# A third segment of layer 0 turned by VectorE, and the long rows put last

## The reference

```python
e = concat(u, i)                      # x through small weights, by rows
h = adj @ (adj.T @ e)                 # layer 0
x = layernorm(x + layernorm(h) * gamma + beta + x)
T1 = adj @ x ; T2 = 2 * (adj @ T1) - x ; T3 = 2 * (adj @ T2) - T1      # layer 1
out = layernorm(x + x @ W0 + T1 @ W1 + T2 @ W2 + T3 @ W3 + bias)
```

## Time and profile before

| | |
|---|---|
| median of three runs | 1171.82 us |
| profiled execution | 1168.52 us, span 1166.7 us |
| TensorE busy | 1082.1 us, 93% |
| VectorE busy | 910.0 us, 78% |
| ScalarE busy | 330.9 us, 28% |
| GpSimd busy | 265.8 us, 23% |
| read from memory | 338.48 MB, 291 GB/s over the span |
| granted TensorE clock | mean 0.992 of full |

### The profile page before, as it was taken

The page is one execution under the profiler, slowest core; times in us unless marked ns, Lnnn a source line. Parts: engine busy times, 40 slices in busy tenths (PEclk is TensorE's granted clock), DMA queues, the critical chain, the costliest instruction groups (busy, mean ns, idle before and its releaser), DMA issues.

```text
span 1166.7 us, 13999 instructions
## 1 busy us (share of the span) xinstructions
PE 1082.1 (93%) x5050; PEld 467.6 (40%) x5050; DVE 910.0 (78%) x942; ACT 330.9 (28%) x592; POOL 265.8 (23%) x428
## 2 busy tenths in 40 slices
PE   6898999999999999868889999999899999988897
PEld 5454444444544544412333333443334444422332
DVE  2797788999989989898777767655577877678885
ACT  1555546645655654501111111000110000001111
POOL 0475735644534533610000000000000000001110
PEclk9999999999999999999999999999999999989999
DMA  9999999999999996999999999999599999999991
GB/s 284 273 292 288 285 278 319 301 297 292 270 287 296 273 284 174 224 298 346 278 347 345 327 322 322 296 288 261 163 319 347 337 335 348 338 282 346 343 333 30
DMA packets 366970, 340.33 MB, mean 292 GB/s; under 512 B 17500, under 2 KB 365700, under 8 KB 366932
## 3 DMA queue, kind: packets, MB, share of 16 engines
q1 hardware_dynamic: 257972, 232.24, 70.7%
q10 hardware_dynamic: 106496, 105.00, 31.0%
q0 software_dynamic: 2464, 2.59, 0.9%
HBM read 338.48 MB, written 1.31 MB: 291 GB/s over the span
## 4 chain that ended last, share of the span: by engine, by line
PE 55%; DVE 13%; SPq 12%; ACT 10%; issue 5%; ACTq 1%; POOL 1%; DMA 1%; DVEq 0%; POOLq 0%
PE bank L1267 26%; ACT terms L842 9%; SPq L378 7%; DVE turned L557 6%; PE bank L1335 5%; SPq L367 5%; PE bank L1280 5%; PE bank L1095 2%; PE bank L1135 2%; PE bank L1123 2%; PE bank L1107 2%; DVE shared L577 2%; PE bank L1147 2%; ACTq L321 1%; PE bank L1313 1%
## 5 line engine op out<-in xcount | busy, mean ns | idle before, releaser
L433 POOL COPY raw<-raw 32x512 f32<-32x512 f32 x320 | 195.3, 610 | 241.5 <-DVE raw L594 201.6
L1267 PE MATMUL bank<-turned,terms 128*128 128x512 f32 x528 | 235.5, 597 | 3.2 <-DVE turned L557 2.7
L577 DVE STREAM_TRANSPOSE shared<-shared 32x512 f32<-32x512 f32 x320 | 224.0, 700 | 4.1
L1095 PE MATMUL bank<-shared 128*64 128x256 f32 x1600 | 207.0, 387 | 10.3 <-DMA shared<-in_adj 10.3
L557 DVE STREAM_TRANSPOSE turned<-shared 128x2048 f32<-128x2048 f32 x70 | 160.2, 2301 | 62.4 <-PE bank L1267 34.2
L557 DVE STREAM_TRANSPOSE turned<-raw 128x2048 f32<-128x2048 f32 x70 | 159.7, 2296 | 52.7 <-PE bank L1267 37.4
L842 ACT COPY terms<-terms 32x512 f32<-32x512 f32 x312 | 192.2, 616 | 5.0 <-DVE terms L587 0.9
L326 POOL DMA_DIRECT2D out<-scratch x32 | 17.4, 551 | 597.2 <-DVE scratch L789 597.0
L1267 PEld LDWEIGHTS bank<-turned,terms 128*128 128x128 f32 x528 | 97.9, 190 | 131.1 <-issue 129.1
L1095 PEld LDWEIGHTS bank<-shared 128*64 128x64 f32 x1600 | 112.8, 137 | 92.0 <-issue 33.7
L1335 PE MATMUL bank<-turned,terms 128*64 128x512 f32 x360 | 97.0, 603 | 21.9 <-DVE turned L557 21.9
(11 more groups left out here) (158 smaller groups left out, 1085.7 us busy)
## 6 DMA issues: line engine op xcount, KB each, us to landing
shared<-in_adj SPq DMA_DIRECT2D x100, 1024.0 KB, 10.6
raw<-in_adj SPq DMA_DIRECT2D x100, 512.0 KB, 10.8
raw<-in_adj ACTq DMA_DIRECT2D x100, 512.0 KB, 12.9
shared<-in_adj SPq DMA_DIRECT2D x100, 512.0 KB, 10.5
shared<-in_adj ACTq DMA_DIRECT2D x100, 512.0 KB, 12.3
raw<-in_adj SPq DMA_DIRECT2D x80, 256.0 KB, 7.6
shared<-in_x SPq DMA_DIRECT2D x5, 256.0 KB, 4.7
xq<-in_x POOLq DMA_DIRECT2D x40, 32.0 KB, 6.0
```

The source lines that it names most:

```text
L433: last = nc.gpsimd.tensor_copy(moved[Q32 * c:Q32 * (c + 1), :, :, Q32 * q:Q32 * (q + 1)], beside[Q32 * q:Q32 * (q + 1), :, c, :, :])
L577: last = nc.vector.transpose(low_turned[Q32 * c:Q32 * (c + 1), :, :, Q32 * q:Q32 * (q + 1)], low[Q32 * q:Q32 * (q + 1), :, :, Q32 * c:Q32 ...
L1095: last = nc.tensor.matmul(t_bank[H * odd:H * (odd + 1), 0:PW], e[:, s * SB + b, :], panels[slot][:, s * SB + b, :], start=(k == 0 and b < ...
L1267: last = nc.tensor.matmul(sum_bank[parity][:, :], terms[:, c * GB + i, columns], turned[place][:, i * BANK:(i + 1) * BANK], start=(first a ...
```

## The change

Segment 1 becomes `THIRD`, and `TILED` becomes 1. The segment is no longer turned by TensorE nor read a second time. VectorE turns it in one instruction per panel (`turn_third`, after `ACROSS`, in place of `turn_last_tile` in every second panel). ScalarE moves blocks 0 to 7 (`move_third`, after the sixteen of `spread_across` and before `keep_t`), GpSimd blocks 8 to 15 (`help_third`, after `move_beside`). TensorE multiplies it in four matmuls at the end of the panel (`add_h_third`), where two `turn_blocks`, two `add_h` and, per two panels, four `add_h_tile` are gone. Its buffers are `raw[1]` and `turned[1]`, so the first load of layer 1 waits for both movers. The segment is loaded again at VectorE's signal. After the last panel ScalarE makes all sixteen spread moves, and GpSimd moves its half of `THIRD` ahead of `BESIDE`. In the second sweep the rows 7 and 8, of eight tiles each, come last instead of early. The second sweep has the same tiles and windows.

```diff
-        TILED = BESIDE
+        TILED = THIRD
-        ROWS3 = [0, 7, 9, 8, 1, 6, 2, 5, 4, 3]
+        ROWS3 = [0, 9, 6, 1, 2, 5, 4, 3, 7, 8]
-        LAST_LOW = [(7, 3), None, (7, 2), (7, 1), (7, 0), (9, 0), (8, 3), (8, 2), (8, 1), (8, 0), (1, 0),
-                    (6, 2), (6, 1), (6, 0), (2, 0), (5, 2), (5, 1), (5, 0), (4, 1), (4, 0), (3, 1), (3, 0)]
+        LAST_LOW = [(6, 2), None, (6, 1), (9, 0), (6, 0), (1, 0), (5, 2), (2, 0), (5, 1), (5, 0), (4, 1), (4, 0),
+                    (3, 1), (3, 0), (7, 3), (7, 2), (7, 1), (7, 0), (8, 3), (8, 2), (8, 1), (8, 0)]
...
-                        sp.wait_ge({BESIDE: beside_made, ACROSS: across_made}.get(k, low_made), uses * 2 + (slot - 1))
+                        sp.wait_ge({THIRD: third_made, BESIDE: beside_made, ACROSS: across_made}.get(k, low_made),
+                                   uses * 2 + (slot - 1))
-                load_panel(0, pair - 1, end - 2 * PW, [(1, (pair - 1) * TILED - 3, end - 2 * BANK)])
+                load_panel(0, pair - 1, end - 2 * PW)
+                if u == 0:
+                    sp.wait_ge(tile_turned, T1 + RAW)
+                    sp.wait_ge(third_moved, NJ)
+                    sp.wait_ge(third_helped, NJ)
...
+            def help_third(j):
+                pool.wait_ge(third_made, j)
+                pool.wait_ge(third_used, j)
+                for block in range(HALF_MOVES, NQ * NQ):
+                    q, c = block // NQ, block % NQ
+                    last = nc.gpsimd.tensor_copy(third_turned[Q32 * c:Q32 * (c + 1), :, :, Q32 * q:Q32 * (q + 1)],
+                                                 third[Q32 * q:Q32 * (q + 1), :, c, :, :])
+                last.then_inc(third_helped, 1)
-            pool.wait_ge(across_made, NJ)
-            pool.wait_ge(spread_used, NJ)
-            for block in range(NQ * NQ // 2, NQ * NQ):
...
+            def turn_third(slot, j, first=False):
+                if not first:
+                    dve.wait_ge(third_moved, j - 1)
+                    dve.wait_ge(third_helped, j - 1)
+                segment = panels[slot][:, SEGS[THIRD] * SB:(SEGS[THIRD] + 1) * SB, :]
+                nc.vector.transpose(third.rearrange("p cc c b i -> p b (cc c) i"),
+                                    segment.rearrange("p b (c i) -> p b c i", i=Q32)).then_inc(third_made, 1)
                 turn_beside(slot, j)
                 turn_across(slot, j)
+                turn_third(slot, j, first)
                 turn_low(slot, j)
-                turn_last_tile(m)
...
+            def move_third(j):
+                act.wait_ge(third_made, j)
+                act.wait_ge(third_used, j)
+                for block in range(HALF_MOVES):
...
                 for i in range(ITEMS):
                     copy_turned(i, (j - 1) * ITEMS)
-                    if i == ITEMS - 2:
-                        spread_across(j, 0, 3)
-                spread_across(j, 3, NQ * NQ)
+                spread_across(j, 0, NQ * NQ)
+                move_third(j)
                 keep_t(slot, j)
...
+            move_third(NJ)
+            for i in range(ITEMS):
+                copy_turned(i, before)
             load_next()
+            spread_across(NJ, 0, 4)
             take_h(0, SEGS[0])
...
             root(0, 2 * GB)
-            spread_across(NJ, 4, NQ * NQ // 2, NQ * NQ // 2)
+            spread_across(NJ, 4, NQ * NQ)
             root(1, 2 * GB)
...
+            def add_h_third(slot, cc, j, stop):
+                if cc == 0:
+                    pe.wait_ge(third_moved, j)
+                    pe.wait_ge(third_helped, j)
+                for gg in range(2):
+                    last = nc.tensor.matmul(h_bank[SEGS[THIRD]][H * gg:H * (gg + 1), :],
+                                            t_cols[:, slot, cc * H:(cc + 1) * H],
+                                            third_turned[:, cc, gg * GB:(gg + 1) * GB, :],
+                                            start=False, stop=stop, skip_group_check=True)
                 for cc in range(PB):
                     add_h_moved(1 - slot, cc, j, False)
+                for cc in range(PB):
+                    add_h_third(1 - slot, cc, j, False)
```

More of the change, by code:

```diff
@@ L50 @@
 SLOTS = 4
+THIRD = 1
 BESIDE = 2
@@ L114, in resnorm_chebyshev @@
         moved = raw_base[:, pair_size + tile_size:2 * pair_size].rearrange("p (cc b r) -> p cc b r", cc=PB, r=P)
+        third = raw[1].rearrange("p (cc c b i) -> p cc c b i", cc=PB, c=NQ, i=Q32)
+        third_turned = turned[1].rearrange("p (cc b r) -> p cc b r", cc=PB, r=P)
         pairs = [raw_base[:, 0:pair_size], shared[:, at + pair_size:at + 2 * pair_size], shared[:, at:at + pair_size],
@@ L469, in _ @@
                 move_beside(j)
-            pool.wait_ge(across_made, NJ)
-            pool.wait_ge(spread_used, NJ)
-            for block in range(NQ * NQ // 2, NQ * NQ):
-                q, c = block // NQ, block % NQ
-                last = nc.gpsimd.tensor_copy(spread[Q32 * c:Q32 * (c + 1), :, :, Q32 * q:Q32 * (q + 1)],
-                                             across[Q32 * q:Q32 * (q + 1), :, c, :, :])
-            last.then_inc(spread_helped, 1)
-            pool.wait_ge(spread_helped, 1)
             pool.wait_ge(tile_used, TURNED + T1)
@@ L615, in center_xq, with beside_panel @@
                 dve.wait_ge(xq_step, g * 3 + 3)
-            def beside_panel(slot, j, m):
+            def beside_panel(slot, j, m, first=False):
                 dve.wait_ge(t_ready, j)
@@ L677, in _ @@
                 beside_group(m, center_two)
-            turn_tile(1, DMA * NQ * NG, 1, T1 - 1 - TILED)
+            dve.wait_ge(seg_loaded[1][SEGS[THIRD]], DMA * (NJ // 2))
+            turn_third(1, NJ)
             dve.wait_ge(seg_loaded[1][SEGS[ACROSS]], DMA * (NJ // 2))
@@ L833, in copy_turned, with spread_across @@
                 nc.scalar.copy(at_turned[i % AT], turn_bank[i % 2][:, :]).then_inc(at_copied, 1)
-            def spread_across(j, first, end, signal=NQ * NQ):
+            def move_third(j):
+                act.wait_ge(third_made, j)
+                act.wait_ge(third_used, j)
+                for block in range(HALF_MOVES):
+                    q, c = block // NQ, block % NQ
+                    last = nc.scalar.copy(third_turned[Q32 * c:Q32 * (c + 1), :, :, Q32 * q:Q32 * (q + 1)],
+                                          third[Q32 * q:Q32 * (q + 1), :, c, :, :])
+                last.then_inc(third_moved, 1)
+            def spread_across(j, first, end):
                 if first == 0:
@@ L843, in spread_across @@
                                           across[Q32 * q:Q32 * (q + 1), :, c, :, :])
-                if end == signal:
+                if end == NQ * NQ:
                     last.then_inc(spread_made, 1)
@@ L925, in load_through @@
                     load_next()
+            before = (NJ - 1) * ITEMS
+            move_third(NJ)
+            for i in range(ITEMS):
+                copy_turned(i, before)
             load_next()
-            before = (NJ - 1) * ITEMS
-            copy_turned(0, before)
-            copy_turned(1, before)
-            copy_turned(2, before)
+            spread_across(NJ, 0, 4)
             take_h(0, SEGS[0])
-            spread_across(NJ, 0, 4)
-            copy_turned(3, before)
             take_y(0, SEGS[0])
@@ L1152, in add_h_moved @@
                     last.then_inc(beside_used, 1)
+            def add_h_third(slot, cc, j, stop):
[7 more added lines that the diff above has]
+                                            start=False, stop=stop, skip_group_check=True)
+                if cc == PB - 1:
+                    last.then_inc(third_used, 1)
             def add_h_tile(k, c, t, stop):
@@ L1242, in _ @@
                 k, cc = UNITS[u - 1]
-                if k == BESIDE:
+                if k == THIRD:
+                    add_h_third(1, cc, NJ, cc == PB - 1)
+                elif k == BESIDE:
                     add_h_moved(1, cc, NJ, cc == PB - 1)
                 elif k == ACROSS:
-                    if cc == 0:
-                        pe.wait_ge(spread_helped, 1)
                     add_h_spread(1, cc, NJ, cc == PB - 1)
```

39 lines of the change are left out of this document (28 added, 11 removed).

## The result

The kernel after takes 1255.62 us, the median of four runs (1253.51 to 1256.42), beside 1173.01 us for four runs of the kernel before. The ratio is 1.0703, with a 95% interval of 1.068 to 1.0726. The prediction was 1233 in a range of 1198 to 1267: right in sign, and 23 us too fast, about as much as one term of the sum, the price of the low clock, missed.

What follows compares the result with a forecast made beforehand. It took ScalarE's chain between panels (22.1 us, TensorE almost as long) as the bound. Layer 0 +62, between layers +6, end -7 give +61 on the profiled 1168.5, so 1229.5, and 3.3 more for the median: 1233, range 1198 to 1267.

Steps and rivals of the forecast that it cites:

- the price of the low clock: Layer 0: slow matmuls after TensorE's wait before combine_t, taken as 1.5 us a panel, 27 us in all.
- The chain between two `t_ready`: Layer 0, one panel's round trip through ScalarE's copies and moves: 24.4 us instead of 22.1, +35 us in all.
- The wait made for TensorE: Layer 0, before combine_t: TensorE idles 3.5 us in each panel until ScalarE has finished t_sum.
- The rival with the stretch twice as long: Layer 0: the clock stays low 6.8 us per panel, costing 3.4 us each; +95 us, so 1267; chance 0.13.
- the case that I took: Layer 0: the clock falls about once a panel for a short stretch, 1.5 us each; 1233 us; chance 0.55.
- The estimate of 31 us: Layer 0, by the Trainium skill: every panel starts at the low clock, 18 x 1.7 us, where the forecast has 27.
- VectorE and GpSimd stay under the chain: Layer 0: VectorE needs 22.2 us a panel and GpSimd at most 21.4, both under the chain's 24.4.
- VectorE and GpSimd in each other's way: Only quarter copies could collide with GpSimd's third-segment moves, once after the last panel: at most 3 us, none in the sum.
- Between the layers: From the last panel of layer 0 to layer 1's first tile: later copies and more ScalarE moves, +6 us, bounds 3 and 10.
- The end: Last rows of the second sweep, reordered: less VectorE waiting and shorter TensorE work after it, -7 us, bounds 0 and -12.
- The sweeps up to the last of the upper rows: Layer 1 up to its last rows: the same length as before, no change.
- The sum: Whole kernel: +62 in layer 0, +6 between the layers, -7 at the end, +61 us together.

Runs made afterwards that it cites:

- experiment 1: The kernel after with 13 unused identity products on TensorE before combine_t in every panel, filling its wait; 1210.82 us, ratio 1.0346 to before.
- experiment 2: The kernel after with six or three unused identity products before combine_t, leaving TensorE waits of 1.96 or 2.63 us; 1215.2 and 1253.58 us.
- experiment 6: The kernel after with keep_t ahead of move_third and the third segment's matmuls in the middle of the next panel; 1170.73 us, ratio 0.9986 to before.
- experiment 3: The kernel after with ScalarE moving 4 of the third segment's 16 blocks instead of 8, GpSimd 12; 1186.83 us, ratio 1.0142 to before.
- experiment 4: The order of the last rows exchanged: the old order in the kernel after, 1266.89 us; the new order alone in the kernel before, 1163.12 us.
- experiments 5 to 7: Kernel after with keep_t before move_third (1181.56 us), also third matmuls deferred (1170.73), GpSimd's last-spread help restored (1250.26), or the deferred version with between-layer lists reordered (1171.31).
- `e7_help`: The kernel after with GpSimd making the second half of the last spread again, as in the kernel before; 1250.26 us, ratio 1.0671 to before.

## Why the forecast was right, and where it was not

- *The chain between two `t_ready`.* Right. The second copy ends 10.34 us after `t_ready` instead of 7.97 (332.51 - 322.17), the 24 moves take 15.06 (305.24 to 320.30; 15.07 forecast), the rest 1.84 (from 320.33) instead of 1.38. Both differences are matmuls at the low clock; without it the panel is 24.31 (experiment 1). 18 x 24.31 = 437.6 of layer 0, 439.2 forecast.
- *The wait made for TensorE.* Right in place and size, 3.49 us.
- *What it costs.* This is the step that failed, "I take 1.5, a short stretch in most panels". Measured: 3.0 a panel (27.31 - 24.31), in all 16 intervals from the fourth on. In layer 0 that is 540.6 - 53.0 - 437.6 = 50.0 us instead of 27, the whole of its miss but for 2 us of the chain in the other direction. The row nearest in size, the wait of 3.11 us with 6.8 us of low clock, gives the right stretch; I set it aside because what followed it was half idle, and here the stretch is as long with full matmuls behind it. But that this row would be right could not be known from its length: the same wait is followed by 6.8 us in four traces, by 3.4 in two and by none in six (experiment 2). The rival with the stretch twice as long, which had a chance of 0.13 against 0.55 for the case that I took, was the true one in its mechanism. It had 3.4 a panel; the measured price is 3.0, most of the difference because some 0.6 us of the low stretch still falls into the wait. The time lies inside the range because the range reached to this rival.
- *The Trainium skill*, "TensorE: Matmul & The Clock Gate", section "HAM oscillation — how this bites in real kernels", says of a loop in which every tile waits some 3 to 5 us for its data that every tile starts at the low clock. After waits of 3.49 us, and here already of 2.63 us, the traces agree in every settled panel, though not in the first ones. With waits of 1.96 us, shorter than those of the page, most panels stayed at full clock. The estimate of 31 us from it used my short stretch and is below the 50 measured.
- *VectorE and GpSimd stay under the chain.* Right in the kernel after; the 44.3 us for two panels were confirmed when the chain was shorter (44.0 to 44.4, experiment 6). GpSimd was never late in a panel of the kernel after.
- *VectorE and GpSimd in each other's way.* The prediction let only the quarter copies collide. The product L642, with two inputs, does so too: beside GpSimd's moves it takes 0.83 instead of 0.42 us in experiment 3. In the kernel after all ten of them take 0.42, so it cost nothing there.
- *Between the layers*: +8.8 instead of +6, and it is the clock again. In this stretch of the kernel after, ScalarE and TensorE:

```profile
548.25 5.01 ACT L867 COPY turned<-raw 32x512 f32<-32x512 f32 x8 [7.64 <-PE bank L1202]
...
553.93 1.12 PE L1157 MATMUL bank<-scratch,t_cols 128*64 128x512 f32 x1 [4.76 <-ACT scratch L859]
...
572.87 0.21 ACT L938 ACTIVATE stats<-stats 128x8 f32<-128x8 f32 x1
...
574.43 2.73 ACTq L328 DMA_DIRECT2D raw<-in_adj  x1
...
582.68 1.08 PE L1392 MATMUL bank<-turned,terms 128*64 128x512 f32 x4
```

  `move_third(NJ)` starts 7.6 after `t_ready` instead of 5.0, TensorE then waits 4.76 us and works at half speed once more (1.12 instead of 0.59), and `root(1)` is at +32.2 instead of +28.4. In experiment 1, where the clock is full from 280 us up to the twentieth `t_ready`, it comes at +29.1 and the first tile at +39.9 (38.7 forecast). The later first load was hidden here: its issue, 2.73 us long, ends at 577.16, and ScalarE waited for TensorE until 577.43 anyway.
- *The end*: -7.1, as forecast, and its parts hold: VectorE from tile 65 (1135.56) to its last turn 104.6 us (104.2 forecast), then 4.3 for TensorE (3.9). VectorE's two waits where rows end two tiles apart:

```profile
1150.91 0.18 DVE L546 RECIPROCAL stats<-stats 128x4 f32<-128x4 f32 x1 [4.56 <-ACT stats L938]
...
1159.10 0.18 DVE L546 RECIPROCAL stats<-stats 128x4 f32<-128x4 f32 x1 [1.71 <-ACT stats L938]
...
1237.91 2.27 DVE L576 STREAM_TRANSPOSE xq<-raw 128x2048 f32<-128x2048 f32 x1
```

  The second one is 1.7 instead of 4.4, so the agreement to a few tenths has some luck in it. The same exchange was worth 5.9 us of the end in before and 12.8 in after (experiment 4). A part of the difference is the clock again: with the old order in after TensorE waits a second time before L1501, 2.95 us, and the granted clock is 0.82 from 1150 to 1170 us, where a low stretch of 10.2 us begins at 1147.1; in before there is no such wait. The rest is open.
- *The sweeps up to the last of the upper rows*: +2.2, forecast as nothing. In experiment 1 it is +0.5. In this stretch the kernel after has two low stretches of 3.4 us, at about 593 and 924 us, experiment 1 has one, and before has none. That they make the difference is likely but wasn't tested.
- *The sum.* The span was forecast as 1227.7: +20.8 in layer 0, +2.8 behind it, +2.2 in the sweeps and -0.1 at the end make 1253.4. The forecast also added 3.3 from the profiled execution to the median; here the two lie 0.4 apart.

Not settled: why the same wait is followed by none, 3.4 or 6.8 us of low clock, so why the first panels of the kernel after are cheaper (24.3 and 26.5 us) and which of the panels with a wait of 1.96 us are hit; and whether the step between 1.96 and 2.63 us belongs to the wait or to this loop, whose chain is 24.3 us in all these runs.

## What to carry to other kernels

Where a change takes work from one engine and puts it in front of another's signal, the freed engine gets a wait, and for TensorE the wait may cost nearly as much again. One row of a wait of the same length is not enough to price it: at some 3.1 us it was none, 3.4 or 6.8 us of low clock. Don't take the middle of such outcomes for a loop either, since a loop can settle on the dearest one in every round: carry both ends through the sum. Such a loop can be tested with one edit, useless products in the wait; if they make it faster, the clock is part of the bill. And before moving work at all, add up the engine that receives it: here VectorE needs 22.0 to 22.2 us a panel (experiment 6), and the kernel before takes 22.1, so there was next to nothing to win in a panel, and none of the later orders that were tried (experiments 5 to 7) made this half of the change pay.

## What the runs showed of the hardware

- TensorE's clock after a wait in a loop that is otherwise full: 0.40 us, none low; 1.96 us, none or 3.4 us low; 2.63 and 3.49 us, none or 3.4 us in the first panels, then 6.8 us low each time, 3.0 us of loss. After a single wait of 3.02 to 3.25 us: none in six traces, 3.4 us in two, 6.8 us in four.
- Small instructions of VectorE can be held while GpSimd works, though its turns are not (2.27 us with GpSimd's moves beside them and without). In the kernel after, a product of 128x64 beside a 2.88 us one of GpSimd:

```profile
261.87 2.88 POOL L493 TENSOR_TENSOR xq<-xq,rows 128x1280 f32<-128x1280 f32 x1
261.92 2.91 DVE L677 TENSOR_TENSOR centres<-centres,rows 128x64 f32<-128x64 f32 x1
...
265.56 0.22 DVE L680 TENSOR_TENSOR w<-w,both 128x64 f32<-128x64 f32 x1
```

  The same size takes 0.22 us alone. The Trainium skill, "SBUF — State Buffer", section "Who interferes with whom", says that an instruction of VectorE with two inputs in SBUF contends with one of GpSimd that reads SBUF; this row agrees with it. It happens a few times in a launch here and decides nothing.
- The issue of a 512 KB load on ScalarE's queue takes 0.3 to 0.5 us in most cases, but the last two of four take 1.79 and 3.43 us in `e7_help`, where ScalarE's next instruction stood behind them for 4.54 us. The same four come as close together in before and take 0.32 to 0.51 each, so closeness alone isn't the cause; what is wasn't tested.
